# A pair's layers, turns and products moved among the lookups of the next pairs in a recommendation tower

## The chip, the cores and the metric

The kernel runs on one core of one Trainium2 chip. The metric is the time of one execution in microseconds (us) of device time, as the median of several runs.

## The reference

The input is a batch of 2048 samples. Each has 27 categorical ids and 16 dense numbers. Each id picks a row of 128 floats from its own table; the products of all pairs of the 27 rows, the dense numbers behind them, go through three layers.

```python
e = jnp.stack([tbl_f[ids[:, f]] for f in range(27)], axis=1)      # (2048, 27, 128)
inter = jnp.einsum('bnd,bmd->bnm', e, e)
i, j = jnp.triu_indices(27, k=1)
h = jnp.concatenate([inter[:, i, j], dense_ctx], axis=1)          # (2048, 367)
h = jnp.maximum(h @ W_top1 + b_top1, 0.0)                         # 512
h = jnp.maximum(h @ W_top2 + b_top2, 0.0)                         # 256
y = h @ W_top3                                                    # (2048, 1)
```

All numbers are float32. Eleven of the tables have 1000 rows; the other sixteen have 1000 to 125000.

## The kernel before

The batch is cut into 8 pairs (`PAIRS`) of two tiles of 128 samples. Every tile needs `emb`: 128 partitions (the embedding's dimension) by 128 samples by 27 features. There are two sources for it.

**Gathered features (16).** POOL issues one indirect DMA for each feature and tile (L609) into a ring of five row banks of four features (four banks a tile). The rows arrive with samples on the partitions and have to be turned. For three of the four halves of a pair, named (p,0,0), (p,0,1) and (p,1,0) by pair, tile and half, VectorE flips blocks of 32 by 32 (`flip_half`, L866, two banks a half); SP stores the half to DRAM (`store_half`, L412) and loads it back with its blocks exchanged in four DMAs (`load_half`, L423); ScalarE copies it into `emb` (`take_half`, L968). There is one flip buffer and one buffer `moved` for all halves, so a store waits for the flip, a load for its store and for the copy of the half before, and a flip for the store of the half before. The last two banks of tile 1 are turned by TensorE (`turn`, L649) and evicted by ScalarE (`take_turned`, L958).

**One-hot features (11).** VectorE compares the ids, broadcast to 125 partitions by SP (`load_ids`, L402), with row numbers and writes one-hot pieces (`make_onehot`, L811) into a ring of three. TensorE multiplies them with a table that lies in two parts in SBUF (`look_up`, L638 and L640). A lookup mostly serves two pairs at once: it has two pieces and 16 matmuls 512 wide, and ScalarE evicts it (`take_lookup`, L936 for the half held back for the next pair, L937). Cycle p of the loop over pairs makes six lookups for p = 1, 3, 5 and five for p = 2, 4, 6; the last cycle (p = 7) makes six of one piece. Three PSUM banks serve lookups and turns.

**Products and layers.** `gram_products` (L668) makes the products of one tile in four turns of two PSUM banks; ScalarE empties each (`take_gram`, L979). SP stores them to DRAM once both tiles are done (`store_products`, L447) and loads them back in the order that layer 1 wants (`load_z`, L486). Layer 1 of pair p-1 (`layer1`, L685, four chunks of six matmuls, two PSUM banks) runs in cycle p, ScalarE evicts each chunk (`take_layer1`, L988); layer 2 (`layer2`, L694) uses the same two banks, and VectorE makes bias, ReLU and the last layer in place (`score`, L848 and L853). SP stores the scores (`store_y`, L491).

**Order.** Each engine has its own instruction stream, written out by hand, and works it off strictly in order; semaphores tie the streams together. Nothing plans the order. In cycle p > 0 the streams before are:

- TensorE: all lookups; layer 1 of pair p-1, four chunks; products of tile 0; turns of tile 1; layer 2 of pair p-1; products of tile 1.
- VectorE: pieces 0 to 2; flip (p,0,0); scores of pair p-2; piece 3; flip (p,0,1); pieces 4 to 7; flip (p,1,0) ahead of piece 8; the rest. In the last cycle, with six pieces, that flip stands behind the last one.
- ScalarE: the held lookups (L949); half (p,0,0); lookups 0 to 3; half (p,0,1); the other lookups; four layer-1 evictions; the products of tile 0; the dense numbers (L1001); the turned banks; half (p,1,0); the products of tile 1.
- SP: two ids loads; store of half (p,0,1); products of pair p-1; load of half (p,0,1); z of pair p-1; dense numbers; ids; store of half (p,1,0); ids; load of half (p,1,0); ids; store and load of half (p+1,0,0); scores of pair p-1.
- POOL: nothing but gathers, each bank once the bank five before it has been flipped or turned.

Of the kernel before, what the change touches and what calls it, by code (L numbers as in the profile page):

```python
# [44 lines left out]
TILES = 2  # L45
# [62 lines left out]
PIECES_BEFORE_FLIP = [0] + [8] * (PAIRS - 3) + [8, 6]  # L108
HALF_AFTER = 4
# [38 lines left out]
def list_banks():  # L148

    out = []  # L150
    for p in range(PAIRS):
        for at, i in enumerate(cycle_lookups(p)):
            out += [("turn", p * TILES + t, n) for t, n in turns_ahead(p, at)]
            out += [("ids", k) for k in shared_ahead(i)]
            out.append(("look", i))
        if p > 0:
            out += [("turn", p * TILES + 1, n) for n in range(HALF_BANKS, TURN_BANKS)]
    return out
# [67 lines left out]
def build(nc, dense_t, ids_rows, ids_onehot, gathered_tables, onehot_tables, w1, w2, w3, b1, b2, out):  # L226
    with ExitStack() as ctx:
# [165 lines left out]
        def _(sp):  # L393
# [221 lines left out]
        def _(pe):  # L615
# [136 lines left out]
            for p in range(PAIRS):  # L752
                for at, i in enumerate(cycle_lookups(p)):
                    for t, n in turns_ahead(p, at):
                        turn(p, t, n)
                    for k in shared_ahead(i):
                        spread_shared(k)
                    look_up(i)
                    if i + len(spread_ps) < NO:

                        spread_ids(i + len(spread_ps))
                    elif i == NO - 2:

                        spread_rows()
                if p > 0:
                    if p == 1:
                        pe.wait_ge(weights_loaded, 2 * 16)

                        pe.wait_ge(rows_placed, 1)

                    pe.wait_ge(z_loaded, p * Z_LOADS * 16)
                    for m in range(M1):
                        layer1(p - 1, m)
                gram_products(p, 0)
                if p > 0:
                    for n in range(HALF_BANKS, TURN_BANKS):
                        turn(p, 1, n)
                    layer2(p - 1)
                gram_products(p, 1)
# [8 lines left out]
        def _(dve):  # L788
# [81 lines left out]
            for p in range(1, PAIRS):  # L870
# [23 lines left out]
        def _(act):  # L894
# [120 lines left out]
            for p in range(PAIRS):  # L1015
                place_held(p)
                if p > 0:
                    take_half(p, 0, 0)
                for at, i in enumerate(cycle_lookups(p)):
                    if p > 0 and at == HALF_AFTER:  # L1020
                        take_half(p, 0, 1)
                    for t, n in turns_ahead(p, at):
                        take_turned(p, t, n)
                    for k in shared_ahead(i):
                        if k > 0:
                            finish_onehot(k)
                    take_lookup(i)
                    if i == NO - 2:

                        act.wait_ge(rows_spread, 1)  # L1030
# [81 lines left out]
```

## Time and profile before

| | |
|---|---|
| median of 3 runs | 366.14 us (365.24 to 367.49) |
| the profiled execution's own time | 367.44 us |
| its span, first to last instruction | 365.6 us |
| mean granted TensorE clock | 0.981 of full speed |
| busy share of the span | PE 90%, PEld 73%, DVE 67%, POOL 66%, ACT 55% |
| matmuls, DVE instructions, ACT instructions | 3310, 202, 294 |
| bytes moved by DMA | 66.07 MB, mean 181 GB/s |

PE is TensorE's matmuls, PEld its weight loads (they overlap), DVE is VectorE, ACT ScalarE, POOL GpSimd; SP is the queue that issues most DMAs. Times in the trace count from the start of the span. A matmul's end is modelled, so the starts of successive matmuls say more than their lengths. A bracket behind an instruction gives the idle time of its engine before it and what ended it. A DMA issue's length is that of the issue, not of the transfer.

### The profile page before, as it was taken

The page shows a single profiled execution, that of the slowest core. Times are in us where ns is not written, and L with a number is a line of the kernel's source. Part 1 is how long each engine was busy: PE and PEld are TensorE (multiplying, and loading weights), DVE is VectorE, ACT ScalarE, POOL GpSimd, SP SyncE. Part 2 cuts the span into 40 slices and gives each one's busy share as a digit, 9 for nine tenths or more (in the row PEclk, how much of TensorE's full clock was granted, in tenths as well). Part 3 has the DMA queues.
Part 4 walks back from the last instruction along what each step waited for, and adds up shares of the span by engine and source line. Part 5 has one row for each costly group of instructions (what it writes and reads, how often), then busy time and mean ns, then how long its engine had stood idle before and what let it go on. Part 6 is the DMA issues. An engine that isn't in the chain of part 4 may idle for free.

```text
span 365.6 us, 7977 instructions
## 1 busy us (share of the span) xinstructions
PE 328.5 (90%) x3310; PEld 267.8 (73%) x3310; DVE 246.0 (67%) x202; ACT 200.5 (55%) x294; POOL 242.6 (66%) x263
## 2 busy tenths in 40 slices
PE   2899899989999899989999899989999899659966
PEld 1667788757886588757986688757986689658865
DVE  6899995999339782999349782999349863810201
ACT  4798966624674357542674357443673457333621
POOL 6777777777677777777677777777677777750000
PEclk9999999999999999999999999999999999887989
DMA  7976893897678988898578778898478766981340
GB/s 170 226 175 149 251 222 112 234 233 210 187 135 208 196 221 203 156 256 224 160 137 213 219 211 186 174 239 243 135 137 226 205 164 175 200 236 59 57 85 0
DMA packets 69101, 66.07 MB, mean 181 GB/s; under 512 B 41490, under 2 KB 56415, under 8 KB 69065
## 3 DMA queue, kind: packets, MB, share of 16 engines
q1 hardware_dynamic: 59113, 48.55, 50.2%
q0 software_dynamic: 8192, 16.79, 22.3%
q8 instruction: 26, 0.43, 0.5%
q10 hardware_dynamic: 1760, 0.22, 0.4%
q14 instruction: 10, 0.08, 0.1%
HBM read 47.44 MB, written 18.10 MB: 179 GB/s over the span
## 4 chain that ended last, share of the span: by engine, by line
PE 66%; DVE 15%; issue 10%; DMA 4%; SPq 2%; ACT 1%; ACTq 0%; DVEq 0%
PE gram_ps L668 15%; PE emb_ps L638 14%; DVE onehot L811 13%; PE emb_ps L640 12%; PE mlp_ps L685 11%; PE mlp_ps L694 7%; PE emb_ps L649 3%; DVE flips L866 2%; PE emb_ps L712 2%; DMA products<-gram 1%; DMA gram<-tbl_rows 1%; DMA z<-products 1%; SPq L447 1%; PE mlp_ps L739 1%; DVE table_lo L832 1%
## 5 line engine op out<-in xcount | busy, mean ns | idle before, releaser
L609 POOL DMA_INDIRECT rows<-tbl_rows,idx x256 | 241.7, 944 | 83.4 <-issue 76.8
L811 DVE TENSOR_TENSOR onehot<-ids_b,row_id 125x2048 fp32r<-125x2048 int32 x72 | 159.9, 2272 | 40.4 <-PE emb_ps L640 32.3
L638 PE MATMUL emb_ps<-onehot,table_hi 125*128 125x512 f32 (+1 forms) x400 | 150.2, 384 | 22.1 <-DVE onehot L811 12.6
L640 PE MATMUL emb_ps<-onehot,table_lo 125*128 125x512 f32 (+1 forms) x400 | 144.2, 369 | 0.0
L638 PEld LDWEIGHTS emb_ps<-onehot,table_hi 125*128 125x128 f32 x400 | 76.9, 192 | 53.5 <-ACT emb L937 15.0
L640 PEld LDWEIGHTS emb_ps<-onehot,table_lo 125*128 125x128 f32 x400 | 77.0, 193 | 10.7
L668 PEld LDWEIGHTS gram_ps<-emb 128*54 128x54 f32 x2048 | 53.6, 130 | 6.3 <-issue 5.2
L668 PE MATMUL gram_ps<-emb 128*54 128x54 f32 x2048 | 55.8, 214 | 1.2 <-ACT emb L937 0.8
L936 ACT COPY held<-emb_ps 128x256 f32<-128x256 f32 x38 | 14.2, 374 | 71.4 <-PE emb_ps L640 71.4
L968 ACT COPY emb<-moved 128x1024 f32<-128x1024 f32 x21 | 43.3, 2061 | 15.5 <-DMA moved<-halves 15.1
L979 ACT COPY gram<-gram_ps 118x432 f32<-118x432 f32 x64 | 33.2, 519 | 28.2 <-PE gram_ps L668 26.8
L685 PE MATMUL mlp_ps<-z,w_sb 126*128 126x256 f32 x168 | 40.3, 398 | 4.0 <-DMA z<-products 4.0
L685 PEld LDWEIGHTS mlp_ps<-z,w_sb 126*128 126x128 f32 x168 | 33.6, 201 | 9.6 <-DMA z<-products 4.2
L937 ACT COPY emb<-emb_ps 128x256 f32<-128x256 f32 x50 | 33.7, 687 | 5.3 <-PE emb_ps L640 5.3
L848 DVE TENSOR_TENSOR mlp_ps<-mlp_ps,rows 128x256 f32<-128x256 f32 x14 | 6.1, 433 | 45.2 <-PE mlp_ps L694 45.2
L811 DVE TENSOR_TENSOR onehot<-z,mlp_ps 125x2048 fp32r<-125x2048 int32 (+1 forms) x16 | 33.5, 2114 | 1.5 <-PE mlp_ps L739 1.1
L866 DVE STREAM_TRANSPOSE flips<-rows 128x512 f32<-128x512 f32 x42 | 27.9, 691 | 8.7 <-DMA rows<-tbl_rows,idx 8.7
L988 ACT ACTIVATE h<-mlp_ps,columns 128x256 f32<-128x256 f32 x28 | 13.3, 473 | 22.4 <-PE mlp_ps L685 22.4
L694 PE MATMUL mlp_ps<-w_sb,h 128*128 128x256 f32 x112 | 25.3, 379 | 0.0
L694 PEld LDWEIGHTS mlp_ps<-w_sb,h 128*128 128x128 f32 x112 | 20.7, 190 | 2.5
L949 ACT COPY emb<-held 128x1280 f32<-128x1280 f32 (+1 forms) x7 | 19.1, 2726 | 0.0
L958 ACT COPY emb<-emb_ps 128x512 f32<-128x512 f32 x22 | 13.6, 652 | 0.1
(51 smaller groups left out, 128.7 us busy)
## 6 DMA issues: line engine op xcount, KB each, us to landing
halves<-flips SPq DMA_DIRECT2D x21, 512.0 KB
moved<-halves SPq DMA_DIRECT2D x84, 128.0 KB
ids_b<-ids_onehot SPq DMA_DIRECT2D x33, 256.0 KB, 6.1
products<-gram SPq DMA_DIRECT2D x28, 216.0 KB, 5.3
gram<-tbl_rows SPq DMA_DIRECT2D x9, 480.0 KB
rows<-tbl_rows,idx POOLq DMA_INDIRECT x256, 4.2
z<-products SPq DMA_DIRECT2D x14, 126.0 KB
h<-tbl_rows SPq DMA_DIRECT2D x2, 480.0 KB
```

What stands on the lines that cost most here:

```text
L609: pool.indirect_dma_start(out=rows[:, bank_number(p, t, n) % ROW_BANKS, f - first, :], out_offset=None, in_=gathered_tables[f], in_offset= ...
L638: nc.tensor.matmul(ps[:, 0:width], table_hi[0:ROWS, k, j, :], columns[:, c, :], start=j == 0, stop=False)
L640: last = nc.tensor.matmul(ps[:, 0:width], table_lo[0:ROWS, k, j, :], columns[:, c, :], start=False, stop=j == ROWS_PER - 1)
L668: last = nc.tensor.matmul(ps[half * HALF_ROWS:half * HALF_ROWS + GRAM_COLS, b * GRAM_COLS:(b + 1) * GRAM_COLS], samples, samples, start=Tr ...
L685: last = nc.tensor.matmul(ps[:, 0:PAIR], w1_sb[0:k, s, m * P:(m + 1) * P], z[0:k, s, :], start=s == 0, stop=s == STEPS - 1)
L694: last = nc.tensor.matmul(mlp_ps[t][:, 0:HID2], h1[:, k, t * P:(t + 1) * P], w2_sb[:, k, :], start=k == 0, stop=k == M1 - 1)
L811: nc.vector.tensor_tensor(onehot[0:ROWS, seq % ONEHOT_RING, 0:own * width].rearrange("p (j b) -> p j b", b=width), *operands, ALU.is_equal ...
L866: nc.vector.transpose(flips[:, :, g, 0:size, :].rearrange("p b f j -> p f b j"), row_bank(p, t, n).rearrange("p f (b i) -> p f b i", b=BLOCKS)
L937: nc.scalar.copy(emb[:, :, :, emb_slot(k)], ps[:, 0:PAIR].rearrange("d (t b) -> d t b", t=TILES)).then_inc(emb_taken, 1)
L949: nc.scalar.copy(emb[:, :, :, slot:slot + size].rearrange("d t b f -> d (t b) f"), held[:, place:place + size, :].rearrange("d f b -> d b ...
L968: nc.scalar.copy(emb[:, t, :, first:first + size].rearrange("d (q j) f -> d q j f", j=BLOCK), moved[:, :, 0:size, :].rearrange("d q f j -> ...
L979: nc.scalar.copy(gram[0:GRAM_PART, :, :, g0:g0 + GROUPS_A_BANK].rearrange("r s j g -> r (s j) g"), gram_ps[a % GRAM_BANKS][0:GRAM_PART, 0: ...
```

## The change

The loop of pairs is written anew on all engines but POOL; no instruction of a pair's work is added or left out, and the tail behind the loop stays.

- TensorE: layer 2 of pair p-2 stands behind the first lookup of cycle p. The first two chunks of layer 1 of pair p-1 stand in front of the last lookup, the other two behind it. Then come the turns of tile 1 and the products of both tiles. In the last cycle the order at the end is products of tile 0, layer 2 of pair 6, turns, products of tile 1.
- VectorE: the scores of pair p-2 and flip (p,0,1) stand before piece 5 (before piece 4 in the last cycle), flip (p,1,0) before piece 10, or behind the last piece where there are only ten or six.
- ScalarE: half (p,0,1) is copied behind all lookups but the last; then two layer-1 evictions, the last lookup, half (p,1,0), the other two evictions, the turned banks, and the products of both tiles with the dense numbers between them. In the last cycle half (p,1,0) and the turned banks stay between the tiles' products.
- SP: products of pair p-1 come ahead of the store of half (p,0,1), z ahead of its load; the scores of pair p-2 (not p-1, and not at the end of the cycle) are stored behind the dense numbers and the ids of this cycle; three ids loads stand ahead of the store of half (p,1,0), whose load follows at once.

The condition on `HALF_NUMBER` holds for every p > 0, since `is_flipped` is not changed.

```diff
@@ -105,8 +105,8 @@
 FLIPPED_HALVES = [(p, t, n // HALF_BANKS) for p, t, n in FLIPPED if n % HALF_BANKS == 0]
 TURNED_BY = {bank: n + 1 for n, bank in enumerate(TURNED)}
 FLIPPED_BY = {bank: n + 1 for n, bank in enumerate(FLIPPED)}
-PIECES_BEFORE_FLIP = [0] + [8] * (PAIRS - 3) + [8, 6]
-HALF_AFTER = 4
+PIECES_BEFORE_SCORE = [0] + [5] * (PAIRS - 2) + [4]
+PIECES_BEFORE_FLIP = 10
 HALF_NUMBER = {half: n for n, half in enumerate(FLIPPED_HALVES)}
...
@@ -522,27 +522,27 @@
 
             for p in range(1, PAIRS):
                 ids, ahead = lookups_of(p)[IDS_SLOTS:], lookups_of(p + 1)[:IDS_SLOTS] if p < LAST else []
-                for i in ids[0:2]:
+                for i in ids[0:1]:
                     load_ids(i)
+                store_products(p - 1)
                 store_half(p, 0, 1)
-                store_products(p - 1)
+                load_z(p - 1)
                 load_half(p, 0, 1)
-                load_z(p - 1)
                 load_dense(p)
-                for i in ids[2:]:
+                for i in ids[1:]:
                     load_ids(i)
-                for i in ahead[0:2]:
+                if p >= 2:
+                    store_y(p - 2)
+                for i in ahead[0:3]:
                     load_ids(i)
-                store_half(p, 1, 0)
-                for i in ahead[2:3]:
-                    load_ids(i)
-                load_half(p, 1, 0)
+                if (p, 1, 0) in HALF_NUMBER:
+                    store_half(p, 1, 0)
+                    load_half(p, 1, 0)
                 for i in ahead[3:]:
                     load_ids(i)
                 if p < LAST:
                     store_half(p + 1, 0, 0)
                     load_half(p + 1, 0, 0)
-                    store_y(p - 1)
...
-                if (p, t, 0) in HALF_NUMBER:
+                if p > 0:
...
-            for p in range(PAIRS):
-                for at, i in enumerate(cycle_lookups(p)):
-                    for t, n in turns_ahead(p, at):
-                        turn(p, t, n)
-                    for k in shared_ahead(i):
-                        spread_shared(k)
-                    look_up(i)
...
-                if p > 0:
-                    if p == 1:
-                        pe.wait_ge(weights_loaded, 2 * 16)
-
-                        pe.wait_ge(rows_placed, 1)
-
-                    pe.wait_ge(z_loaded, p * Z_LOADS * 16)
-                    for m in range(M1):
-                        layer1(p - 1, m)
-                gram_products(p, 0)
-                if p > 0:
-                    for n in range(HALF_BANKS, TURN_BANKS):
+            def look_ahead(p, at):
...
+                look_up(i)
...
+            def turn_second(p):
+                for n in range(TURN_BANKS):
+                    if not is_flipped(p, 1, n):
                         turn(p, 1, n)
+
+            for at in range(NO):
+                look_ahead(0, at)
+            gram_products(0, 0)
+            gram_products(0, 1)
+            for p in range(1, PAIRS):
+                looks = len(cycle_lookups(p))
+                for at in range(looks - 1):
+                    look_ahead(p, at)
+                    if at == 0 and p > 1:
+                        layer2(p - 2)
+                if p == 1:
+                    pe.wait_ge(weights_loaded, 2 * 16)
+
+                    pe.wait_ge(rows_placed, 1)
+
+                pe.wait_ge(z_loaded, p * Z_LOADS * 16)
+                for m in range(M1):
+                    if m == M1 // 2:
+                        look_ahead(p, looks - 1)
+                    layer1(p - 1, m)
+                if p < LAST:
+                    turn_second(p)
+                    gram_products(p, 0)
+                    gram_products(p, 1)
+                else:
+                    gram_products(p, 0)
                     layer2(p - 1)
-                gram_products(p, 1)
+                    turn_second(p)
+                    gram_products(p, 1)
...
-                if p >= 2:
-                    for t in range(TILES):
-                        score(p - 2, t)
                 for at, (i, part) in enumerate(pieces[ONEHOT_RING:], ONEHOT_RING):
-                    if at == ONEHOT_RING + 1:
+                    if at == PIECES_BEFORE_SCORE[p]:
+                        if p >= 2:
+                            for t in range(TILES):
+                                score(p - 2, t)
                         flip_half(p, 0, 1)
-                    elif at == PIECES_BEFORE_FLIP[p]:
+                    elif at == PIECES_BEFORE_FLIP and (p, 1, 0) in HALF_NUMBER:
                         flip_half(p, 1, 0)
                     make_onehot(i, part)
-                if PIECES_BEFORE_FLIP[p] >= len(pieces):
+                if len(pieces) <= PIECES_BEFORE_FLIP and (p, 1, 0) in HALF_NUMBER:
                     flip_half(p, 1, 0)
...
-            for p in range(PAIRS):
                 place_held(p)
-                if p > 0:
-                    take_half(p, 0, 0)
-                for at, i in enumerate(cycle_lookups(p)):
-                    if p > 0 and at == HALF_AFTER:
-                        take_half(p, 0, 1)
...
-                    take_lookup(i)
...
+            def take_ahead(p, at):
+                i = cycle_lookups(p)[at]
...
+                take_lookup(i)
...
+            def take_second(p):
+                for n in range(TURN_BANKS):
+                    if not is_flipped(p, 1, n):
+                        take_turned(p, 1, n)
+
...
+            for p in range(1, PAIRS):
+                looks, chunk = len(cycle_lookups(p)), (p - 1) * MLP_CHUNKS
...
-                chunk = (p - 1) * MLP_CHUNKS
-                if p > 0:
-                    for m in range(M1):
+                take_half(p, 0, 0)
+                for at in range(looks - 1):
+                    take_ahead(p, at)
+                take_half(p, 0, 1)
+                for m in range(M1 // 2):
+                    take_layer1(chunk, m)
+                take_ahead(p, looks - 1)
+                if p < LAST:
+                    if (p, 1, 0) in HALF_NUMBER:
+                        take_half(p, 1, 0)
+                    for m in range(M1 // 2, M1):
                         take_layer1(chunk, m)
-                if p == 0:
-
-                    act.wait_ge(table_split, NO * GRAM_BANKS)
-                take_gram(p, 0)
-                if p < LAST:
+                    take_second(p)
+                    take_gram(p, 0)
                     place_dense(p)
-                if p > 0:
-                    for n in range(HALF_BANKS, TURN_BANKS):
-                        take_turned(p, 1, n)
+                    take_gram(p, 1)
+                else:
+                    for m in range(M1 // 2, M1):
+                        take_layer1(chunk, m)
+                    take_gram(p, 0)
                     take_half(p, 1, 0)
-                take_gram(p, 1)
+                    take_second(p)
+                    take_gram(p, 1)
 
```

## Rows read from the trace of the kernel before

**Rows 1.** Windows: length, busy time (instructions) of each engine, clock, DMA.

```profile
105.79:144.42 38.63, 36.55 (x385) 29.47 (x385) 27.71 (x22) 21.54 (x29) 29.18 (x32) 1.00 0.83 199
144.42:187.45 43.03, 40.72 (x402) 32.33 (x401) 32.01 (x24) 22.06 (x31) 31.20 (x34) 1.00 0.81 194
307.77:347.32 39.55, 32.74 (x401) 29.72 (x400) 11.13 (x13) 18.75 (x25) 14.41 (x16) 0.87 0.61 143
```

**Rows 2.** Waits, whole run: us in total, times, longest.

```profile
PE emb_ps L638 <- DVE onehot L811: 12.6, 21, 1.4
```

**Rows 3.** Timeline of DVE in the cycle of pair 3: start, us, instruction.

```profile
146.57 2.29 DVE L811 TENSOR_TENSOR onehot<-ids_b,row_id 125x2048 fp32r<-125x2048 int32 x1 [4.53 <-PE emb_ps L640]
...
149.99 8.84 DVE L811 TENSOR_TENSOR onehot<-ids_b,row_id 125x2048 fp32r<-125x2048 int32 x4
...
158.76 1.28 DVE L866 STREAM_TRANSPOSE flips<-rows 128x512 f32<-128x512 f32 x2
...
182.38 0.43 DVE L848 TENSOR_TENSOR mlp_ps<-mlp_ps,rows 128x256 f32<-128x256 f32 x1 [4.96 <-PE mlp_ps L694]
```

**Rows 4.** Timeline of PE, first matmul of the second lookup of that cycle.

```profile
148.11 0.39 PE L638 MATMUL emb_ps<-onehot,table_hi 125*128 125x512 f32 x1
```

**Rows 5.** Chain in order of time, the same cycle: start, us, what.

```profile
170.97 5.20 PE mlp_ps L685 x24
...
176.17 3.42 PE gram_ps L668 x128
...
180.61 3.46 PE mlp_ps L694 x16
```

**Rows 6.** Timeline of ACT, the same cycle.

```profile
171.28 0.69 ACT L937 COPY emb<-emb_ps 128x256 f32<-128x256 f32 x1
...
174.91 0.47 ACT L988 ACTIVATE h<-mlp_ps,columns 128x256 f32<-128x256 f32 x1 [0.82 <-PE mlp_ps L685]
...
180.74 1.17 ACT L958 COPY emb<-emb_ps 128x512 f32<-128x512 f32 x2
...
181.93 1.98 ACT L968 COPY emb<-moved 128x1024 f32<-128x1024 f32 x1
...
185.06 0.52 ACT L979 COPY gram<-gram_ps 118x432 f32<-118x432 f32 x1 [1.15 <-PE gram_ps L668]
```

**Rows 7.** Timeline of SP: DMA issues of halves and products.

```profile
59.91 0.33 SPq L412 DMA_DIRECT2D halves<-flips  x1
...
63.30 2.58 SPq L423 DMA_DIRECT2D moved<-halves  x4
...
163.60 0.43 SPq L412 DMA_DIRECT2D halves<-flips  x1
...
171.09 1.76 SPq L423 DMA_DIRECT2D moved<-halves  x4
...
302.45 0.34 SPq L412 DMA_DIRECT2D halves<-flips  x1
...
305.36 2.66 SPq L423 DMA_DIRECT2D moved<-halves  x4
...
313.89 4.82 SPq L447 DMA_DIRECT2D products<-gram  x4
```

**Rows 8.** Timeline of ACT: copies of a half that waited for its load.

```profile
69.35 2.08 ACT L968 COPY emb<-moved 128x1024 f32<-128x1024 f32 x1 [3.49 <-DMA moved<-halves]
...
313.97 1.94 ACT L968 COPY emb<-moved 128x1024 f32<-128x1024 f32 x1 [3.19 <-DMA moved<-halves]
```

**Rows 9.** Timeline of PE in the last cycle.

```profile
316.52 0.58 PE L638 MATMUL emb_ps<-onehot,table_hi 125*128 125x256 f32 x1 [2.80 <-ACT emb L937]
...
319.68 0.28 PE L638 MATMUL emb_ps<-onehot,table_hi 125*128 125x256 f32 x1
...
327.87 8.13 PE L685 MATMUL mlp_ps<-z,w_sb 126*128 126x256 f32 x24 [3.96 <-DMA z<-products]
```

**Rows 10.** Window in the last cycle; the clock is the figure before DMA.

```profile
317.00:318.00 1.00, 1.00 (x7) 1.00 (x7) 1.00 (x2) 0.49 (x1) 0.92 (x1) 0.50 1.08 253
```

More of the change, by code:

```diff
@@ L156, in list_banks @@
         if p > 0:
-            out += [("turn", p * TILES + 1, n) for n in range(HALF_BANKS, TURN_BANKS)]
+            out += [("turn", p * TILES + 1, n) for n in range(TURN_BANKS) if not is_flipped(p, 1, n)]
     return out
@@ L751, in _ @@
                 spread_ids(k)
-            for p in range(PAIRS):
-                for at, i in enumerate(cycle_lookups(p)):
-                    for t, n in turns_ahead(p, at):
-                        turn(p, t, n)
-                    for k in shared_ahead(i):
-                        spread_shared(k)
-                    look_up(i)
[L759 to L764, printed above, removed]
-                if p > 0:
-                    if p == 1:
-                        pe.wait_ge(weights_loaded, 2 * 16)
-                        pe.wait_ge(rows_placed, 1)
-                    pe.wait_ge(z_loaded, p * Z_LOADS * 16)
-                    for m in range(M1):
-                        layer1(p - 1, m)
-                gram_products(p, 0)
-                if p > 0:
-                    for n in range(HALF_BANKS, TURN_BANKS):
-                        turn(p, 1, n)
+            def look_ahead(p, at):
+                for t, n in turns_ahead(p, at):
+                    turn(p, t, n)
+                i = cycle_lookups(p)[at]
+                for k in shared_ahead(i):
+                    spread_shared(k)
+                look_up(i)
+                if i + len(spread_ps) < NO:
+                    spread_ids(i + len(spread_ps))
+                elif i == NO - 2:
+                    spread_rows()
@@ L1014, in _ @@
                     finish_onehot(0)
-            for p in range(PAIRS):
-                place_held(p)
-                if p > 0:
-                    take_half(p, 0, 0)
-                for at, i in enumerate(cycle_lookups(p)):
-                    if p > 0 and at == HALF_AFTER:
-                        take_half(p, 0, 1)
[L1022 to L1026, printed above, removed]
-                    take_lookup(i)
-                    if i == NO - 2:
-                        act.wait_ge(rows_spread, 1)
-                        nc.scalar.copy(rows23[:, :, :].rearrange("p n h -> p (n h)"), rows_ps[:, :]
-                                       ).then_inc(rows_placed, 1)
-                    if i + 2 < NO:
-                        show_table(i + 2)
-                    if i + ahead < NO:
-                        round_table(i + ahead)
-                chunk = (p - 1) * MLP_CHUNKS
-                if p > 0:
-                    for m in range(M1):
+            def take_ahead(p, at):
+                i = cycle_lookups(p)[at]
+                for t, n in turns_ahead(p, at):
+                    take_turned(p, t, n)
+                for k in shared_ahead(i):
+                    if k > 0:
+                        finish_onehot(k)
+                take_lookup(i)
+                if i == NO - 2:
+                    act.wait_ge(rows_spread, 1)
+                    nc.scalar.copy(rows23[:, :, :].rearrange("p n h -> p (n h)"), rows_ps[:, :]
+                                   ).then_inc(rows_placed, 1)
+                if i + 2 < NO:
+                    show_table(i + 2)
+                if i + ahead < NO:
+                    round_table(i + ahead)
@@ new lines, in take_second @@
+            def take_second(p):
+                for n in range(TURN_BANKS):
+                    if not is_flipped(p, 1, n):
+                        take_turned(p, 1, n)
+            for at in range(NO):
+                take_ahead(0, at)
+            act.wait_ge(table_split, NO * GRAM_BANKS)
+            take_gram(0, 0)
+            place_dense(0)
+            take_gram(0, 1)
+            for p in range(1, PAIRS):
+                looks, chunk = len(cycle_lookups(p)), (p - 1) * MLP_CHUNKS
+                place_held(p)
+                take_half(p, 0, 0)
[9 more added lines that the diff above has]
+                    for m in range(M1 // 2, M1):
```

## The prediction

> **What bounds the kernel now.** I read the stretches first, one for each cycle of the loop over pairs [rows 1]. Six-lookup cycles (pairs 1, 3, 5) last 43.03 us with TensorE busy for 40.72, five-lookup cycles (2, 4, 6) 38.63 with 36.55, the last cycle 39.55 with 32.74. So TensorE sets the pace, and about 2.2 us of each middle cycle are lost. The waits say where: at the lookups' first matmuls it waits for one-hots from VectorE [rows 2]. A ring of three pieces lies between the two. VectorE needs 2.2 us a piece (8.84 for four, [rows 3]), TensorE about 1.85 (the second lookup starts 3.7 us after the first, [rows 4]), and the order now puts all lookups in one row, then 5.20 us of layer 1, then 3.42 + 1.02 + 3.46 + 3.4 us of products, turns and layer 2 [rows 5], during which VectorE can run only three pieces ahead. The reader should see a busy engine with a badly placed 15 us block, and beside it a second chain that is now hidden: each flipped half goes VectorE, store to DRAM, load, ScalarE copy. That chain is what I price, since the change moves it most.
>
> **The change, on a clock that starts with the cycle.** Pieces 0 to 2 are ready at 0, as now. VectorE's third piece starts at 2.15 (146.57 against the cycle's start at 144.42, [rows 1, 3]), pieces 3 and 4 end at 6.6.
>
> VectorE's scores now stand before piece 5. They need layer 2 of the pair two back, which TensorE does behind lookup 0, from 3.7 to 7.2; two scores of two 0.43 us passes and a readout take about 1.0 us each [rows 3], so they end at 8.5 and wait for nothing. Flip (p,0,1), 1.3 us for two banks, ends at 9.8; pieces 5 to 9 end at 20.7; flip (p,1,0) now stands before piece 10 (in five-lookup cycles behind the last piece) and ends at 22.0. Today the same flip ends at 160.04, 15.6 us after the cycle's start.
>
> TensorE: the gaps do fill. Lookup 1 runs 7.2 to 11.0, lookup 2 to 14.7, lookup 3 to 18.6. In a five-lookup cycle two layer-1 chunks (2.6) end at 21.2 and the last lookup at T = 25.0; in a six-lookup cycle lookup 4 ends at 22.8, the chunks at 25.4, the last lookup at T = 29.2 (pieces 10 and 11 are done at 24.2 and 26.4, in time). Then two chunks (2.6), turns (1.0), two tiles' products (6.8): T + 10.4, and about 0.6 more because ScalarE must first place a half, so 40.2 and 36.0 if nothing else is late.
>
> ScalarE: here is what is late. Its new order after the last lookup is half (p,1,0), layer-1 evictions 2 and 3, two turned banks, and only then the first product bank. Before, this half was copied between the two tiles' products (181.93, 37.5 us after the cycle's start, [rows 6]) with nothing waiting. Now ScalarE is free for it at about T + 1.3: 30.5 in a six-lookup cycle, 26.3 in a five-lookup one. From the flip's end at 22.0 that leaves 8.5 and 4.3 us for store and load. TensorE has two product banks: it fills both by T + 5.3 (34.5 and 30.3) and then stands until ScalarE has emptied one. After the landing come the half's copy 2.0, two evictions 0.9, two turned banks 1.2, the first product copy 0.5 [rows 6], and six banks of 0.85 (3.42 for four): 9.8 us with handovers. The cycle lasts 22.0 + R + 9.8, R being the round trip.
>
> R: the trace has no round trip for this half, since ScalarE never waited for it; I bound it by those it did wait for. From the store's issue to ScalarE's start it was 9.4 us at 59.91 and 11.5 at 302.45 [rows 7, 8]. By legs: the store of this very half took 7.5 us (163.60 to 171.09), with ids loads issued just ahead of it; the shortest load leg was 6.05 (63.30 to 69.35), the other 8.6 (305.36 to 313.97) [rows 7, 8]. So R lies between 9.4 and 16.1. In the new order three to four ids loads and the scores' store are still issued in the 5 us ahead of this store, but the z load lies 10 us ahead instead of 4; I take 11.5, the measured whole trip nearest to such a stretch. That gives 43.3.
>
> The clock: with R = 11.5 TensorE idles from 30.3 or 34.5 to 22.0 + 11.5 + 4.6 = 38.1, so 7.8 or 3.6 us. Idle stretches of 2.80 and 3.96 us in the last cycle were each followed by matmuls at a granted 0.50, the 1.2 GHz level [rows 9, 10]: 3.16 us of it cost half, 1.6; layer 1 took 8.13 instead of 5.20, so 2.9 [rows 5, 9]. None of the middle cycles has this (granted 1.00, [rows 1]). I take 2.2, the middle; bounds 1.6 and 2.9, and none where the idle stays below 2.8. A middle cycle becomes 45.5 us.
>
> Last cycle: the products' stores begin at about 1.0 us, behind the last product copy and one ids load, not behind the flip (313.89, 6.1 us after the start, [rows 7]), so z, which came 14.0 us after that, arrives at about 15.0 instead of 20.1 (327.87, [rows 9]). Its lookups are half as wide and five of them plus layer 2 end at 13.1; the wait shrinks to 1.9, with no slow clock by the rows above. Half a layer 1, lookup, the other half held up 1.2 by half (7,0,1), products, layer 2, turns, products: 15.0 + 2.6 + 1.9 + 1.2 + 2.6 + 3.4 + 3.5 + 1.0 + 3.4 = 34.6, so -4.9 against 39.55; at worst -1.5 if z comes late and the clock falls.
>
> Costed at nothing: SP's other moves. z is needed at 18.6 at the earliest in a middle cycle and comes, by the same 14.0 us, at about 15 to 17; if products take long this cover of two us goes, and the half's store behind it on SP slips too. The scores' store is moved in front of three ids loads and this half's store: no wait, but some more packets in its way, inside R. POOL's gathers are not moved; they wait longer for row banks, in cycles that are longer too. Cycle 1 has no layer 2 and no scores, so its flip is 2 us earlier, but SP reaches the store later; I count it as a six-lookup cycle. The tail is untouched.
>
> **Sum**: three five-lookup cycles 3 x (45.5 - 38.63) = +20.6; three six-lookup cycles 3 x (45.5 - 43.03) = +7.4; last cycle -4.9: +23.1. Against the profiled execution, 367.44 (span 365.6), that is 390.5; it lies 1.3 above the median of 366.14, so the forecast for the median is 389.
>
> **Rivals.** *Full rings*: the store keeps its 7.5 and the load its best 6.05, R = 13.55: 45.4 + 2.2 = 47.6 a cycle, 3 x 9.0 + 3 x 4.6 - 4.9 = +35.9, time 402; with the long load leg (R = 16.1) 417. For it: this half's own store row. Against: today's store stands closer behind z and another half's loads. Chance 0.15.
>
> *Quiet rings* (the other side, not slower): the ids loads have drained, the half comes home in 2.9 (302.45 to 305.36) + 6.05 = 8.95. Six-lookup cycles then end at 40.75 without a slow clock, five-lookup ones at 40.75 + 2.2 = 42.95: 3 x 4.3 - 3 x 2.3 - 4.9 = +1.1, time 367. The point that decides is R of about 8.7, below which the sum is negative. For it: both legs were seen once each, with no ids load just ahead. Against: never together. Chance 0.15, a third of it on the fast side of 1%. The Trainium skill's page "DMA: Bandwidth & Descriptors" (Anatomy of one DMA) fits a DMA by a fixed 2.0 us plus its bytes at 436 GB/s; by that a half's store of 512 KB would be an estimated 3.2 us, the trip with 1.75 us of issue about 8.2, and the time about 363. The trace agrees only for the 2.9 us store; its middle-cycle store took 7.5.
>
> *The half is no obstacle*: it is flipped or taken earlier than I read, and only the filled gaps count: 40.2 and 36.0, so 3 x -2.8 + 3 x -2.6 - 4.9 = -21, time 345. For it: 2.2 us of idle and one layer 2 among the lookups do fit. Against: both engines work in their written order, and a trip of 4.3 us stands in no row. Chance 0.06.
>
> **Chances.** The forecast has 0.64; its own range, R from 9.4 without a slow clock in six-lookup cycles (+4) to 13 with 2.9, is 370 to 402, and some 0.05 of it falls within 1% of the time before. One per cent either way is about what a measurement of this kernel can tell. Faster: 0.06 + 0.05 = 0.11. Same: nearly all the rest of the quiet case and those 0.05, 0.14. Slower: 0.75. The range from 362 to 404 leaves out the no-obstacle case and the far ends of both others, under 2 in 10.
>
> **What would show it.** Right: ScalarE's copies from the moved half waiting for DMA in every middle cycle, some 3 us (six lookups) and 7 (five); TensorE idle in the middle of tile 0's products, with a granted clock below 1.00 behind it; both kinds of cycle about equally long, near 45 us; hardly any wait of the lookups on one-hots; a last cycle near 35. Wrong: product banks following each other without a gap, five-lookup cycles under 39 us, or a round trip under 9 us.

## The result, and the profile after

The changed kernel takes 386.35 us (median of 3 runs, 385.21 to 387.12) against 366.14: ratio 1.0544 [1.0477, 1.0611]. Forecast were 389 us, with 362 to 404 as the range and 0.75 for slower. The profiled span is 384.6 us against 365.6, so 19.0 us have to be found.

First the stretches, cut at the first lookup of each cycle; the columns are those of [rows 1]. The cycle of pair 2 (five lookups), of pair 3 (six), the last one, the part behind it, and two short stretches for the clock; the last line is the part behind the last cycle in the kernel before.

```profile
106.85:148.72 41.87, 36.50 (x388) 31.74 (x385) 27.25 (x22) 20.76 (x29) 31.38 (x34) 0.92 0.73 190
148.72:198.82 50.10, 41.52 (x401) 35.43 (x401) 31.76 (x24) 21.10 (x31) 35.84 (x39) 0.90 0.72 171
...
327.00:365.40 38.40, 33.71 (x416) 30.95 (x416) 12.72 (x19) 19.39 (x24) 11.39 (x13) 0.96 0.51 128
365.40:384.60 19.20, 13.15 (x70) 11.92 (x70) 0.98 (x4) 4.12 (x12) 0.00 (x0) 0.82 0.21 41
...
142.00:145.00 3.00, 3.00 (x66) 3.00 (x68) 0.00 (x0) 0.85 (x2) 2.37 (x3) 0.50 0.98 237
191.00:196.00 5.00, 4.83 (x104) 4.83 (x106) 0.00 (x0) 2.29 (x6) 3.78 (x5) 0.50 0.72 183
...
347.32:365.60 18.28, 11.95 (x70) 10.80 (x70) 0.98 (x4) 3.77 (x12) 0.00 (x0) 0.91 0.22 43
```

TensorE's busy time is about what it was [rows 1], 36.50 and 41.52 against 36.55 and 40.72, although part of it now runs at 0.50, the 1.2 GHz level; in this view nearly all of each cycle's growth is idle time. All six middle cycles: six lookups 44.08, 50.10 and 45.59 us, five lookups 41.82, 41.64 and 40.92. Against 43.03 and 38.63 that is +10.7 and +8.5; the last cycle gives -1.1, and the part behind it +0.9 (19.20 against 18.28): together the 19.0.

The waits of the whole run answer to [rows 2].

```profile
ACT emb L988 <- DMA moved<-halves: 40.2, 10, 8.4
...
PE gram_ps L668 <- ACT gram L999: 32.0, 6, 8.4
...
DVE onehot L831 <- DMA ids_b<-ids_onehot: 9.5, 3, 7.6
...
PE emb_ps L638 <- DVE onehot L831: 4.6, 7, 2.6
```

The lookups' wait for one-hots fell from 12.6 to 4.6 us, so the change does what it is for. In its place stand 32.0 us in which TensorE waits for a free product bank, six times, once in each middle cycle, and behind them ScalarE waiting for the loaded half.

That chain in the cycles of pairs 2 and 3, engine by engine. SP's queue (these answer to [rows 7]; the two rows from 335.33 are of the last cycle):

```profile
128.65 0.33 SPq L412 DMA_DIRECT2D halves<-flips  x1
132.33 2.08 SPq L423 DMA_DIRECT2D moved<-halves  x4
...
164.71 4.84 SPq L402 DMA_DIRECT2D ids_b<-ids_onehot  x3
170.43 0.33 SPq L412 DMA_DIRECT2D halves<-flips  x1
180.85 1.76 SPq L423 DMA_DIRECT2D moved<-halves  x4
...
335.33 2.54 SPq L486 DMA_DIRECT2D z<-products  x3
...
340.39 0.42 SPq L402 DMA_DIRECT2D ids_b<-ids_onehot  x1
```

ScalarE (answering to [rows 6, 8]):

```profile
137.78 1.93 ACT L988 COPY emb<-moved 128x1024 f32<-128x1024 f32 x1 [5.42 <-DMA moved<-halves]
...
186.99 1.92 ACT L988 COPY emb<-moved 128x1024 f32<-128x1024 f32 x1 [8.42 <-DMA moved<-halves]
188.81 0.83 ACT L1008 ACTIVATE h<-mlp_ps,columns 128x256 f32<-128x256 f32 x2
189.54 1.18 ACT L978 COPY emb<-emb_ps 128x512 f32<-128x512 f32 x2
190.58 0.96 ACT L999 COPY gram<-gram_ps 118x432 f32<-118x432 f32 x2
```

TensorE; the rows from 341.45 are of the last cycle and answer to [rows 9]:

```profile
141.96 6.76 PE L668 MATMUL gram_ps<-emb 128*54 128x54 f32 x192 [5.37 <-ACT gram L999]
...
180.99 1.81 PE L668 MATMUL gram_ps<-emb 128*54 128x54 f32 x64
191.17 7.65 PE L668 MATMUL gram_ps<-emb 128*54 128x54 f32 x192 [8.37 <-ACT gram L999]
...
341.45 2.86 PE L685 MATMUL mlp_ps<-z,w_sb 126*128 126x256 f32 x12 [1.24 <-DMA z<-products]
...
346.89 0.43 PE L638 MATMUL emb_ps<-onehot,table_hi 125*128 125x256 f32 x1 [2.58 <-DVE onehot L831]
```

VectorE: the flip of this half, and the last lookup's piece.

```profile
169.12 1.29 DVE L886 STREAM_TRANSPOSE flips<-rows 128x512 f32<-128x512 f32 x2
...
344.45 2.29 DVE L831 TENSOR_TENSOR onehot<-ids_b,row_id 125x2048 fp32r<-125x2048 int32 x1 [7.60 <-DMA ids_b<-ids_onehot]
```

Read pair 3 across the four views. The flip ends at 170.41, the store goes out at 170.43 and its load 10.4 us later, at 180.85; by 182.8 TensorE has filled both product banks (64 matmuls) and stops. ScalarE, free since 178.6, stands in front of the half until 186.99, and only behind the half, two evictions and two turned banks comes the first product copy. The 192 products left take 7.65 us instead of 5.13 (1.5 times [rows 5]'s 3.42 for 128). Pair 2 is the same with a shorter trip: 128.65 to 137.78.

### The profile page after: what moved, and what is told of

Same layout as the page of the kernel before. It is cut to its first block, busy times and chain, and to the rows that moved or that the text cites. A ratio compares the mean times of both kernels' runs of the same rounds, so it can differ in the third digit from the quotient of the medians.

```text
span 384.6 us, 7976 instructions
## 1 busy us (share of the span) xinstructions
PE 329.8 (86%) x3310; PEld 281.3 (73%) x3310; DVE 243.6 (63%) x202; ACT 196.8 (51%) x294; POOL 242.6 (63%) x263
## 4 chain that ended last, share of the span: by engine, by line
PE 32%; DVE 20%; DMA 20%; issue 17%; ACT 6%; SPq 4%; ACTq 0%; DVEq 0%
DVE onehot L831 14%; PE gram_ps L668 13%; DMA halves<-flips 10%; DMA moved<-halves 6%; PE emb_ps L638 6%; PE emb_ps L640 5%; DVE flips L886 3%; SPq L423 2%; ACT emb L978 2%; PE emb_ps L712 2%; ACT gram L999 1%; DMA products<-gram 1%; ACT h L1008 1%; DMA ids_b<-ids_onehot 1%; DMA gram<-tbl_rows 1%
## 5 line engine op out<-in xcount | busy, mean ns | idle before, releaser
L668 PE MATMUL gram_ps<-emb 128*54 128x54 f32 x2048 | 65.9, 234 | 33.8 <-ACT gram L999 32.0
L668 PEld LDWEIGHTS gram_ps<-emb 128*54 128x54 f32 x2048 | 63.6, 150 | 36.8 <-ACT gram L999 33.4
L640 PEld LDWEIGHTS emb_ps<-onehot,table_lo 125*128 125x128 f32 x400 | 77.5, 194 | 11.5
L988 ACT COPY emb<-moved 128x1024 f32<-128x1024 f32 x21 | 42.2, 2011 | 40.4 <-DMA moved<-halves 40.2
L685 PE MATMUL mlp_ps<-z,w_sb 126*128 126x256 f32 x168 | 38.8, 379 | 1.2 <-DMA z<-products 1.2
L685 PEld LDWEIGHTS mlp_ps<-z,w_sb 126*128 126x128 f32 x168 | 31.8, 190 | 6.2 <-DMA z<-products 1.5
L694 PEld LDWEIGHTS mlp_ps<-w_sb,h 128*128 128x128 f32 x112 | 21.1, 190 | 3.0
L929 ACT COPY gram_ps<-table_hi 125x512 f32<-125x512 f32 x22 | 13.3, 642 | 0.1
```

The lines of the kernel that those rows point to most:

```text
L640: last = nc.tensor.matmul(ps[:, 0:width], table_lo[0:ROWS, k, j, :], columns[:, c, :], start=False, stop=j == ROWS_PER - 1)
L668: last = nc.tensor.matmul(ps[half * HALF_ROWS:half * HALF_ROWS + GRAM_COLS, b * GRAM_COLS:(b + 1) * GRAM_COLS], samples, samples, start=Tr ...
L685: last = nc.tensor.matmul(ps[:, 0:PAIR], w1_sb[0:k, s, m * P:(m + 1) * P], z[0:k, s, :], start=s == 0, stop=s == STEPS - 1)
L694: last = nc.tensor.matmul(mlp_ps[t][:, 0:HID2], h1[:, k, t * P:(t + 1) * P], w2_sb[:, k, :], start=k == 0, stop=k == M1 - 1)
L988: nc.scalar.copy(emb[:, t, :, first:first + size].rearrange("d (q j) f -> d q j f", j=BLOCK), moved[:, :, 0:size, :].rearrange("d q f j -> ...
```

## The experiments

All eight edits start from the changed kernel. The kernel before was timed on the same chip each time (medians 366.68, 367.34 and 367.38).

**1. The half's copy back between the tiles' products.**

```diff
                 if p < LAST:
-                    if (p, 1, 0) in HALF_NUMBER:
-                        take_half(p, 1, 0)
                     for m in range(M1 // 2, M1):
                         take_layer1(chunk, m)
                     take_second(p)
                     take_gram(p, 0)
                     place_dense(p)
+                    take_half(p, 1, 0)
                     take_gram(p, 1)
```

> The changed kernel with one move undone: in the middle cycles ScalarE copies half (p,1,0) between the products of tile 0 and tile 1, as it did before the change; all else stays. Theory (the half stands too early in ScalarE's order, and its round trip is the cost): tile 0's products no longer wait, the half is copied at about 36.5 us of a six-lookup cycle and 32.5 of a five-lookup one, the cycles take about 42.3 and 38.2 us instead of 46.6 and 41.5, and the time falls from 386 to about 362. Rival (the lookups with layers between them, or the traffic, are slower by themselves): the cycles stay above 41 and 44, the time above 375.

369.26 us, ratio to the kernel before 1.0076 [1.0036, 1.0115]: about 17 of the 20 us are gone by moving one call in ScalarE's order, and ScalarE waits for this half in none of the six cycles. That is the chain shown. But it does not go below the kernel before as the theory wanted (362). TensorE in pair 1 and the clock around it:

```profile
99.82 4.81 PE L668 MATMUL gram_ps<-emb 128*54 128x54 f32 x128 [3.29 <-ACT emb L988]
```

```profile
95.00:97.00 2.00, 1.52 (x62) 1.39 (x56) 0.71 (x1) 1.34 (x3) 1.50 (x2) 1.00 0.25 68
100.00:102.00 2.00, 2.00 (x47) 2.00 (x47) 0.00 (x0) 0.41 (x1) 1.51 (x2) 0.50 0.55 158
```

The half is there in time now, and its copy itself (1.92 us, with the dense copy ahead of it) leaves TensorE idle for 3.3 us between the tiles in each of six cycles, 19.7 us in all. In five of them a granted 0.50 follows, and the 128 products take 4.8 to 6.1 us; in pair 3 the clock stays at 1.00 behind the same idle, and they take 3.45. In the kernel before turns and layer 2 stood there.

**2. The ids loads for the next cycle behind the half's store and load.** Does the length of the trip come from what is queued ahead of it?

```diff
-                for i in ahead[0:3]:
-                    load_ids(i)
-                if (p, 1, 0) in HALF_NUMBER:
-                    store_half(p, 1, 0)
-                    load_half(p, 1, 0)
-                for i in ahead[3:]:
+                store_half(p, 1, 0)
+                load_half(p, 1, 0)
+                for i in ahead:
                     load_ids(i)
```

> The changed kernel with one move on SP: the ids loads for the next cycle stand behind the store and load of half (p,1,0), not three of them in front. Theory (the loads in front lengthen the half's round trip, 13.2, 16.6 and 13.1 us in six-lookup cycles against 9.1, 8.7 and 8.4): the trip falls to about 9 us in all, six-lookup cycles from 46.6 to about 42.4, five-lookup ones stay near 41.5, the time falls to about 374. Rival (the trip is long from the half loads and z before it): trips unchanged, time 384 to 388.

374.58 us, 1.0208 [1.0117, 1.0298], as forecast. The trip in the six-lookup cycles fell from 13.2, 16.6 and 13.1 us to at most 8.7, 11.3 and 8.7, and these cycles to 41.69, 42.74 and 40.51; in the five-lookup cycles, whose trips had been 8.4 to 9.1, nothing was won: trips of 8.9 to 10.6, cycles of 41.47, 44.20 and 42.21. Pair 3 in SP's queue and on ScalarE, then the waits:

```profile
167.61 0.33 SPq L412 DMA_DIRECT2D halves<-flips  x1
173.70 2.21 SPq L423 DMA_DIRECT2D moved<-halves  x4
```

```profile
178.94 2.06 ACT L985 COPY emb<-moved 128x1024 f32<-128x1024 f32 x1 [1.16 <-DMA moved<-halves]
```

```profile
DVE onehot L828 <- DMA ids_b<-ids_onehot: 62.7, 9, 11.5
...
PE gram_ps L665 <- ACT gram L996: 15.5, 6, 5.2
```

The store takes 6.1 us instead of 10.4, and TensorE's wait at the product banks is halved, 32.0 to 15.5. VectorE now waits 62.7 us for ids instead of 9.5, but little of that reaches TensorE, whose wait for one-hots is 4.2 us. In pairs 1 and 5 the store is no longer what holds the load: SP issued it 0.07 us after ScalarE had copied half (p,0,1) out of `moved` (86.50 and 86.57 in pair 1).

**3. The flip two pieces earlier.**

```diff
-PIECES_BEFORE_FLIP = 10
+PIECES_BEFORE_FLIP = 8
```

> The changed kernel with flip (p,1,0) before piece 8 instead of piece 10, that is 4.2 us earlier on VectorE. Theory: five-lookup cycles get the half 4.2 us earlier and lose most of their stall, from 41.5 to about 36.5 us; in six-lookup cycles SP stands in front of the store at the third ids load, which waits for piece 9, so they change by under 1 us; time about 370. Rival (SP's order does not hold the store): both kinds gain 4 to 6 us, time about 355.

380.79 us, 1.0365 [1.0279, 1.045]: a miss, 370 had been expected. Pair 2, in SP's queue and on ScalarE:

```profile
121.29 1.38 SPq L402 DMA_DIRECT2D ids_b<-ids_onehot  x3
123.05 0.33 SPq L412 DMA_DIRECT2D halves<-flips  x1
130.53 1.76 SPq L423 DMA_DIRECT2D moved<-halves  x4
```

```profile
135.50 1.94 ACT L988 COPY emb<-moved 128x1024 f32<-128x1024 f32 x1 [4.35 <-DMA moved<-halves]
```

The cycle starts at 105.64. The store goes out 17.4 us later instead of 21.8, but takes 7.5 us instead of 3.7, and ScalarE starts the half 29.9 us after the cycle's start, against 30.95 in the changed kernel. All three five-lookup cycles agree: 29.9, 30.8 and 29.0 against 30.95, 30.5 and 30.2. What was gained at the issue was lost on the way. Three 256 KB ids loads stand 1.8 us ahead of the store, and z and half (2,0,1) in the 5.6 us ahead of those; which of them costs the time this run does not show. Most of what the run won against the changed kernel lies in pair 3, 46.32 us instead of 50.10. In the prediction's clock R is not a constant that is added to the flip's end.

**4. Fillers where TensorE idles.** How much of the loss is the slow clock? TensorE gets matmuls with nobody waiting for them ahead of the third product bank of tile 0, into a bank that is free; their results are not read.

```diff
+                    if 0 < p < LAST and t == 0 and i == GRAM_BANKS:
+                        spare = emb_ps[BANK_INDEX[("look", cycle_lookups(p)[-1])] % EMB_BANKS]
+                        for k in range(FILLERS):
+                            samples = emb[:, t, 0:ABREAST, :].rearrange("d s f -> d (s f)")
+                            nc.tensor.matmul(spare[0:GRAM_COLS, 0:GRAM_COLS], samples, samples,
+                                             start=True, stop=True)
```

> The changed kernel with 160 extra small matmuls (the products' shape, into a bank that nobody reads) in each middle cycle, behind the second product bank, where TensorE waits for ScalarE; some 4.3 us at full clock. Theory (the wait also costs clock: products behind it took 6.6 to 7.7 us for 192 matmuls instead of 5.1): the granted clock stays at 1.00 but in the cycle of pair 3, the time falls by 7 to 9 us to about 378. Rival (products behind the wait are paced by ScalarE, not by the clock): time 385 to 388.

With 160 of them 438.37 us, 1.1981 [1.189, 1.2071]: the fillers took 16.0 us a cycle where 4.3 were meant, and became the bound. The tile of the spare bank in pair 1, then, in the repeat with 80 that write to the two halves of the bank in turn (`spare[r0:r0 + GRAM_COLS, ...]`, `r0 = k % HALVES * HALF_ROWS`), fillers and products of pair 3. The records are two for a filler.

```profile
L664 PE MATMUL emb_ps<-emb x320: 213/213/213, 96.5 to 112.5; 128*54 128x54 f32 x160
```

```profile
179.20 4.17 PE L665 MATMUL emb_ps<-emb 128*54 128x54 f32 x160
185.88 6.76 PE L676 MATMUL gram_ps<-emb 128*54 128x54 f32 x192 [2.51 <-ACT gram L1007]
```

> The changed kernel with 80 extra small matmuls in each middle cycle behind the second product bank, now alternating between the two halves of the bank as the products do: 160 records of 26.7 ns, 4.3 us, which is about as long as TensorE waits there (the first filler took 16.1 us, 50 ns a record, and lengthened the cycles). Theory (the wait also costs clock, 1.4 to 2.5 us a cycle): the granted clock stays at 1.00 in all middle cycles but that of pair 3, the products behind the wait take 5.1 us, the time falls by 7 to 9 us to about 378. Rival (products behind the wait are paced by ScalarE): time 385 to 388.

The repeat took 377.06 us, 1.0211 [1.0119, 1.0303], as forecast: 9 us less than the changed kernel, by added work alone. Did the half come sooner? ScalarE still waits for it as long:

```profile
135.61 2.06 ACT L996 COPY emb<-moved 128x1024 f32<-128x1024 f32 x1 [4.68 <-DMA moved<-halves]
```

The six trips are 12.7, 8.4, 14.6, 9.6, 13.1 and 9.1 us (127.18 to 135.61 in pair 2), together 1.7 less than in the changed kernel. The rest lies behind the half's landing, where the granted clock is now 1.00 in every middle cycle but that of pair 3. From the landing to the cycle's end it takes 9.6 us in five cycles (135.61 to 145.21), against 10.7 to 11.8 in the changed kernel; only in pair 3, where 2.51 us of idle are left and the products still take 6.76, is it 11.0. Together that is 7.0 us, the clock's part of the loss.

**5. Experiments 2 and 3 together.**

> The changed kernel with both SP's ids loads behind the half's store and load, and flip (p,1,0) before piece 8. Apart, the first gave 374.6 and the second 380.8, in which the half's trip grew from 8.7 to 12.4 us in five-lookup cycles. Theory A (the trip is long because of bytes already queued, the z and half loads among them): the half lands only 1 to 2 us earlier than with the ids move alone, time 370 to 375, VectorE's waits for ids stay. Theory B (only the ids loads hold it): the trip stays near 9.6 us, the half lands 4.2 us earlier, the stall goes, time about 360.

377.36 us, 1.0273 [1.0217, 1.033]; 370 to 375 had been expected. The trips are 11.75 to at most 14.4 us, and ScalarE starts the half 29.7 to 32.3 us after the cycle's start in five-lookup cycles (30.7 to 32.4 in experiment 2) and 30.0 to 33.0 in six-lookup ones (28.9 to 33.1). The earlier flip again buys nothing. The ids come later still. Below their wait stand rows of pair 3, in SP's queue and on ScalarE:

```profile
DVE onehot L828 <- DMA ids_b<-ids_onehot: 66.5, 10, 12.5
```

```profile
163.87 0.43 SPq L412 DMA_DIRECT2D halves<-flips  x1
173.05 1.75 SPq L423 DMA_DIRECT2D moved<-halves  x4
```

```profile
170.96 2.02 ACT L985 COPY emb<-moved 128x1024 f32<-128x1024 f32 x1
```

The trip has a second obstacle here that neither theory had: the load also waits for ScalarE's copy of half (p,0,1) out of `moved`, which the change put behind all lookups but the last. In pair 3 that copy ended at 172.98 and the load went out at 173.05; pair 1 is the same (86.86 and 86.93). In all six cycles SP stood 4.3 to 8.7 us behind the store before the copy had ended. So this run does not tell how long the trip would be by the queued bytes alone.

**6. Experiment 1 with the dense copy ahead of tile 0's products**, so that only the half's copy stands between the tiles.

```diff
                     take_second(p)
+                    place_dense(p)
                     take_gram(p, 0)
-                    place_dense(p)
                     take_half(p, 1, 0)
```

> The kernel with half (p,1,0) between the tiles' products (369.3 us), and ScalarE's copy of the dense numbers (0.65 us) moved from there to in front of tile 0's products, where ScalarE has time. TensorE's wait between the tiles, 3.28 us in each middle cycle and followed by a granted clock of 0.50, becomes about 2.6 us. Theory (idle stretches of 2.6 us do not cost clock, those of 2.8 and more do): clock 1.00 in the middle cycles, 0.65 + 1.5 us saved in each of six, time about 356. Rival (the clock falls all the same): 0.65 each, time about 365.

The median is 365.99 us, but from 360.62 to 371.29, too scattered for a ratio. The trace is clearer: the idle between the tiles falls by the 0.66 us of the dense copy, 3.28 to 2.61 where the half is home in time. In pairs 2 and 4 it is not (2.77 and 4.73 us of idle), so the half's trip still costs something. What follows the idle differs:

```profile
266.83 5.00 PE L668 MATMUL gram_ps<-emb 128*54 128x54 f32 x128 [2.61 <-ACT emb L988]
...
306.18 3.43 PE L668 MATMUL gram_ps<-emb 128*54 128x54 f32 x128 [2.61 <-ACT emb L988]
```

The same idle, the same 128 products: 5.00 us in one cycle, 3.43 in another. Behind the 2.77 us of pair 2 they took 3.43 too, so the length of the idle alone does not decide; the theory's line between 2.6 and 2.8 us is not there.

**7. Experiment 6, and in the last cycle the ids of the last lookup ahead of the products' stores.**

```diff
-                for i in ids[0:1]:
+                first = 2 if p == LAST else 1
+                for i in ids[0:first]:
                     load_ids(i)
...
-                for i in ids[1:]:
+                for i in ids[first:]:
```

> The same, and in the last cycle SP issues the ids of the last lookup ahead of the products' stores instead of behind z and a half. In the changed kernel VectorE waited 7.6 us for them there and TensorE 2.6 us for the last one-hot. Theory (this is why the last cycle took 38.4 us instead of the forecast 34.6): the wait goes and with it some slow clock, 3 to 4 us less than without this edit, about 353. Rival (z or half (7,0,1) ends last there anyway): no more than 1 us.

362.07 us, 0.9837 [0.9781, 0.9892]: faster than both kernels. In SP's queue the store of the last half, in the cycle that starts at 309.41, and the stretches of that cycle and of the part behind it (the cut lies 0.5 us behind the cycle's last product):

```profile
323.96 0.43 SPq L412 DMA_DIRECT2D halves<-flips  x1
```

```profile
309.40:344.90 35.50, 32.33 (x420) 29.70 (x416) 12.64 (x19) 19.68 (x25) 14.05 (x15) 1.00 0.67 154
344.90:360.50 15.60, 10.32 (x70) 9.16 (x70) 0.98 (x4) 3.33 (x12) 0.00 (x0) 0.97 0.25 46
```

Without the ids wait the flip of the last half is stored at 14.6 us into the cycle instead of 21.1, the clock stays at 1.00, and the cycle lasts 35.0 us to its last product; the part behind it runs at 0.97 and, at 16.1 us, is 2.2 shorter than in the kernel before. Experiment 6, without this move, has 38.0 and 15.8 us there: by these two traces the move is worth 3.0 us, and the shorter part behind the cycle is not its doing. All of the gain on the kernel before lies in these two stretches: this run's middle cycles (42.72, 37.81, 46.78, 37.80, 44.40, 37.79) come to 2.3 us more than three times 43.03 and 38.63. In pair 3 the half was late again (4.76 us of idle, products of 5.85).

**8. Experiment 7 with layer 2 of the pair back between the tiles' products.** Is layer 2 worth more there, as cover for the half's copy, than behind lookup 0?

```diff
                 for at in range(looks - 1):
                     look_ahead(p, at)
-                    if at == 0 and p > 1:
-                        layer2(p - 2)
...
                     gram_products(p, 0)
+                    layer2(p - 1)
                     gram_products(p, 1)
```

> The version with the half's copy back between the products, the dense copy ahead of them and the last cycle's ids load moved up, and besides: TensorE's layer 2 of the pair back between the two tiles' products, where the kernel before had it, instead of behind the first lookup. Nothing is left out. Theory A (layer 2 is worth more as cover): TensorE has 3.4 us of work while ScalarE copies the half (2.0 us), so the idle of about 2.6 us between the tiles goes, and with it the half clock that follows some of them; six cycles shorter by 2.6 to 4, but lookups wait for one-hots again by up to 1 us a cycle: 345 to 356 us. Rival B (layer 2 is worth the same in both places): what the idle gives back returns as waits on one-hots behind lookup 0, whose gap it filled: 358 to 364 us, and the lookups' wait on one-hots is back near 12 us.

365.01 us, 0.9917 [0.9886, 0.9949]: the rival, no gain against experiment 7. The end of pair 3 and the start of pair 4 on TensorE, and the waits:

```profile
181.18 3.72 PE L695 MATMUL mlp_ps<-w_sb,h 128*128 128x256 f32 x16
184.83 3.44 PE L669 MATMUL gram_ps<-emb 128*54 128x54 f32 x128
...
200.01 0.50 PE L639 MATMUL emb_ps<-onehot,table_hi 125*128 125x512 f32 x1 [2.45 <-DVE onehot L831]
```

```profile
PE emb_ps L639 <- DVE onehot L831: 17.4, 13, 2.5
```

The 2.61 us between the tiles are gone and the products follow without a gap. In their place 2.45 us stand in the next cycle's lookups. The five-lookup cycles take 38.8 us instead of 37.8, the six-lookup ones 43.8, 43.3 and 43.3 instead of 42.7, 46.8 and 44.4. Layer 2 fills one of the two holes; where it is put decides mainly which one.

## Why the prediction was right

The mechanism and its place were as written: ScalarE in its order ahead of the products, two full product banks, TensorE idle in the middle of tile 0, a low granted clock behind it. Experiment 1 shows it by itself. Not all of its signs came: ScalarE waited 4.7 to 5.4 us for the half in five-lookup cycles and 3.9, 8.4 and 5.0 in six-lookup ones, not 7 and 3; the two kinds of cycle were not equally long; and two trips (8.7 and 8.4) were under the 9 us named as a sign of being wrong. By steps:

- **Gaps at the one-hots**: the wait fell to 4.6 us, as the schedule of pieces and lookups said. The flip of (p,1,0) ends 21.8 us after the cycle's start in pairs 2 and 3 (22.0 forecast).
- **R, one value of 11.5 for all cycles**: mis-sized, and wrong in being one. Five-lookup cycles measured 9.1, 8.7 and 8.4, the condition of the rival *quiet rings*; six-lookup cycles 13.2, 16.6 and 13.1, that of *full rings*. The bounds 9.4 to 16.1 were missed on both sides. The choice of 11.5 rested on two of the six trips that ScalarE waited for in the trace before; the other four, with the products' stores between store and load, took 12.6 to 13.3 us (150.09 to 162.64 in pair 3). In a six-lookup cycle SP issues four ids loads, and three of them take until 169.55, 0.9 us ahead of the store at 170.43. Experiment 2 moved them and the store took 6.1 us. The Trainium skill's page "DMA: Bandwidth & Descriptors" (Anatomy of one DMA) gives its fit for DMAs issued from GpSimd, while SP issues the half's. The five-lookup cycles come within 0.9 us of the 8.2 that the prediction estimated by it, the six-lookup ones lie 4.9 us or more above.
- **From landing to the cycle's end, 9.8 + 2.2**: measured 10.8, 10.9, 11.8, 11.2, 10.7 and 10.7. Experiment 4's repeat, without the slow clock, gives 9.6 for the first term, so the second is 1.1 to 2.2, 1.4 in the mean: over-sized, with its lower bound of 1.6 above the mean. Its condition, none where the idle stays below 2.8, did not hold: in experiment 6 the clock fell behind 2.61.
- **Sum of the cycles**: five lookups averaged 41.5 instead of 45.5, six lookups 46.6: 12.1 less and 3.3 more than forecast.
- **Last cycle, -4.9**: failed, -1.1. z came 14.5 us after the start as forecast (15.0), and its wait was 1.24. The failed step is "costed at nothing: SP's other moves". The load of the last lookup's ids now stands behind z, half (7,0,1) and dense, and goes out at 340.39; VectorE waited 7.60 us for it, TensorE 2.58, and the lookup's matmuls behind were at 0.43 us each instead of 0.28 [rows 9]. Experiment 7 moved that one load and the cycle took 35.0, where the prediction had 34.6 and experiment 6, without the move, 38.0.
- **Tail "untouched"**: +0.9, at a granted 0.82 instead of 0.91.

So 23.1 - 12.1 + 3.3 + 3.8 + 0.9 = 19.0. That the total came within 3 us rests in part on errors of opposite sign, which is luck. What remains above the kernel before once the chain is gone (1.0076 in experiment 1) is, by the 19.7 us of idle between the tiles, the copy that layer 2 and the turns no longer cover; the prediction said only that the copy used to stand there "with nothing waiting".

Left open: what decides whether 2.61 us of idle (3.27 in experiment 1) are followed by the low clock, why the part behind the last cycle has 0.82 in the changed kernel and 0.99 in experiment 6, and why pair 3 has the longest trip (16.6 us, and 14.6 with the fillers) of the six-lookup cycles. That the ids loads ahead of the store lengthen it was shown by moving all four, not one by one.

## What to carry to other kernels

When work is gathered to fill a gap, look on every other engine for what the scattered work had covered: here a copy that waited for nobody came to stand ahead of the first result that TensorE needed. Price a round trip through DRAM cycle by cycle, by what is issued just ahead of it (here 8.4 to 9.1 us in one kind of cycle, 13.1 to 16.6 in the other) and by when the buffer that it lands in comes free; issuing it earlier behind the same bytes, or to a buffer that is still full, did not bring it home earlier. A filler moved from one hole to another is worth only the difference between the holes (2.61 against 2.45 us here, 1.0 us a five-lookup cycle), so close the hole, or leave the filler where it is.

## What the runs showed of the hardware

- A store issued 4.4 us earlier in its cycle landed 0.6 us earlier (experiment 3, pair 2: the load that waits for it went out 24.9 us after the start instead of 25.5).
- Fillers of 128x54, two records each, came at one record every 50 ns into the same half of one bank (320 in 16.0 us), and every 26 ns into the two halves in turn (160 in 4.17 us), both at a granted 1.00, although each record shows 213 ns.
- Idle stretches of the same 2.61 us were followed by 128 products in 5.00 us and in 3.43 us within one run (experiment 6).
